# A decoder with routed experts: one fill of unused rows dropped, the buffer moved, full blocks taken first, block loads split over two queues

## The reference, cut to what matters

```python
H, I, E = 256, 256, 8      # width, hidden width, experts
# z: the layer-normed tokens (4 * 512 rows of 256); one expert a token
logits = z @ Wg + bg                        # rows x 8, the largest one is chosen
e = argmax(logits)
out = x + gelu(z @ W1[e] + b1[e]) @ W2[e] + b2[e]
```

## Time and profile before

| | us |
|---|---|
| median of 3 runs | 2154.18 (2151.05 to 2156.48) |
| the profiled execution | 2155.8 |
| its span, first to last instruction | 2154.1 |
| PE busy | 1856.0 (86%) |
| DVE busy | 1631.2 (76%) |
| ACT busy | 1281.1 (59%) |
| POOL busy | 218.6 (10%) |

### The profile page before, as it was taken

One profiled execution on the slowest core, in us unless ns is written; L12 is line 12 of the kernel. 1 busy time (PEld: TensorE's weight loads), 2 busy tenths in 40 slices (PEclk: granted clock), 3 DMA queues, 4 the chain that ended last, 5 costly groups with the idle time before them and its releaser, 6 DMA issues.

```text
span 2154.1 us, 41917 instructions
## 1 busy us (share of the span) xinstructions
PE 1856.0 (86%) x17110; PEld 1031.9 (48%) x17110; DVE 1631.2 (76%) x2621; ACT 1281.1 (59%) x1919; POOL 218.6 (10%) x230
## 2 busy tenths in 40 slices
PE   4999988988999988988899978989899987468947
PEld 2576752324666652423666653323567663023224
DVE  8888878796888878696888768697778878339643
ACT  5666646487566656487566645668566645346912
POOL 1000001300100001300100001020100002003413
PEclk8999999999999999999999999999999999689978
DMA  7477710011477730010367640000277761942034
GB/s 273 74 126 118 133 50 12 9 46 31 82 123 126 125 65 12 9 45 21 79 121 124 115 91 12 9 26 21 62 123 124 124 117 30 127 64 101 2 88 107
DMA packets 454607, 169.51 MB, mean 79 GB/s; under 512 B 428389, under 2 KB 444016, under 8 KB 453904
## 3 DMA queue, kind: packets, MB, share of 16 engines
q1 hardware_dynamic: 449216, 149.29, 34.7%
q0 software_dynamic: 5200, 17.55, 4.9%
HBM read 45.14 MB, written 18.52 MB: 30 GB/s over the span
## 4 chain that ended last, share of the span: by engine, by line
PE 48%; DVE 27%; DMA 12%; ACT 6%; issue 4%; SPq 2%; POOL 1%; POOLq 0%; DVEq 0%; ACTq 0%
DVE nmx L2177 14%; DMA arena<-arena 11%; PE ps L753 8%; PE ps L755 8%; PE ps L754 7%; PE ps L1135 6%; PE ps L1121 3%; PE ps L925 3%; DVE arena L1987 3%; PE ps L919 2%; PE ps L920 2%; PE ps L1085 1%; ACT arena L1497 1%; PE ps L1145 1%; SPq L597 1%
## 5 line engine op out<-in xcount | busy, mean ns | idle before, releaser
L2177 DVE TENSOR_REDUCE nmx<-ps 128x2 f32<-128x1024 f32 x384 | 445.1, 1218 | 51.6 <-PE ps L1085 49.8
L1669 ACT ACTIVATE arena<-ps 128x512 f32<-128x512 f32 x768 | 406.8, 601 | 99.9 <-PE ps L1121 94.9
L1972 DVE TENSOR_SCALAR_CACHE_REDUCE ps<-ps 128x1536 f32<-128x1536 f32 x128 | 225.7, 1763 | 46.4 <-PE ps L755 45.6
L1135 PE MATMUL ps<-arena 128*17 128x256 f32 x3072 | 242.8, 393 | 0.0
L1987 DVE SCALAR_TENSOR_TENSOR arena<-arena,rs 128x1536 f16<-128x1536 f32 x128 | 231.6, 1809 | 4.2 <-ACT arena L1559 4.2
L1559 ACT ACTIVATE arena<-arena,rs 128x1536 f16<-128x1536 f32 x128 | 200.8, 1569 | 42.9 <-DVE rs L1978 42.9
L1121 PE MATMUL ps<-arena 64*128 64x512 f16 x768 | 171.0, 396 | 47.7 <-DMA arena<-arena 45.8
L1550 ACT ACTIVATE arena<-ps,nm 128x1536 f32<-128x1536 f32 x128 | 197.0, 1539 | 15.7 <-DVE ps L1972 15.7
L753 PE MATMUL ps<-arena 128*128 128x512 f16 (+2 forms) x508 | 178.5, 352 | 24.7 <-DMA arena<-zx_d 22.6
L919 PE MATMUL ps<-arena 128*128 128x128 f16 x1536 | 185.3, 219 | 0.8 <-DMA arena<-arena 0.8
L920 PE MATMUL ps<-arena 128*128 128x128 f16 x1536 | 185.3, 219 | 0.0
(11 more groups left out here) (334 smaller groups left out, 3553.7 us busy)
## 6 DMA issues: line engine op xcount, KB each, us to landing
zx_d<-in_eye POOLq DMA_DIRECT2D x7, 1300.0 KB
arena<-in_weights SPq DMA_DIRECT2D x8, 929.0 KB, 18.2
arena<-arena SPq DMA_DIRECT2D x72, 64.0 KB, 2.1
arena<-arena SPq DMA_TRANSPOSE x272, 3.7
arena<-in_ctx SPq DMA_DIRECT2D x4, 1024.0 KB, 5.5
arena<-in_ctx_t SPq DMA_DIRECT2D x4, 1024.0 KB, 4.9
arena<-in_experts SPq DMA_DIRECT2D x1, 3840.0 KB, 11.5
arena<-zx_d SPq DMA_DIRECT2D x23, 132.0 KB, 2.2
```

Source lines behind the costliest of these rows:

```text
L1135: mm(ps[32 * j:32 * j + VW, 7, cols], v17[:, kt, 4 * g_ + j, :], pr_[:, (4 * t + j) % RING, cols], start=(kt + half == 0), stop=(kt == mod ...
L1669: A(pr_[:, n % RING, :], ps[:, 4 + n % 3, :], ACT.Exp).then_inc(b_exp.sem, 1)
L1972: TS_(s_, s_, -XS, None, ALU.mult, ALU.min, accum_out=nm[:, i:i + 1]).then_inc(s_max.sem, 1)
L2177: V.tensor_reduce(nmx[:, g_ % 2, ch, :, pp, i], ps[:, 2 * (z % 2):2 * (z % 2) + 2, :], AX.X, ALU.max, negate=True)\
```

## The change

It has six parts.

- `pad_regions` is gone. In its place SP writes, once and before batch 0's x is loaded, one constant row (all 4096.0, which is no token number) to the first 128 rows of each of the 8 regions, by 8 DMAs. Every expert's rows now start behind these 128 (`held` starts at 128), and `REGION` is 2176 rows and no longer 2432.
- A block that isn't full now ends at the last row of its expert and so reads older rows at its front. `above` gives those rows a number past the end, and the scatter leaves them out.
- `arena` is allocated first and not last. Its first byte in a partition moves from 130528 to 16512. That is 224 above a multiple of 256 before, and 128 above one after; or 32 above a multiple of 64, and on one. `b2` moves into it. The small tables of the experts move into `rope_k`, so that they can be written earlier.
- Five blocks (`OLD`) are surely full with rows of batches 0 to 2: 1536 rows less at most 7 unfinished blocks leave 5. Their table is made by `old_blocks` during batch 3's `cross_attention`, they are loaded as soon as buffers are free, and blocks 0 and 1 are computed ahead of batch 3's routing, blocks 2 to 4 beside or behind it. `new_blocks` makes the table of the other 18.
- Batch 3's z is turned by PE (`transpose_last`, 8 products, ACT copies, DVE subtracts) and not by DMA. Its copy of x (L507 before) is issued behind the first three block transposes.
- SP issues only the block transposes; the plain loads are issued from ACT between the gelus (`load_rows`), three blocks ahead, each behind its wait for the buffer. The row numbers are loaded into registers in two lots (5 and 18) on SP, ACT and PE, and no more one a block.

```diff
-PAD = (NE - 1) * P
-REGION = (B - 1) * S + PAD
+OLD = (B - 1) * S // P - (NE - 1)
+REGION = B * S + P
...
+        arena = sb("arena", [P, ARENA // 4])
         wh, wl = sb("wh", [P, NW], F16), sb("wl", [P, NW], F16)
...
             sp.wait_ge(pad_out.sem, 16)
+            sp.wait_ge(pads_set.sem, 15)
+            for e in range(NE):
+                sp.dma_start(zx_d[REGION * e:REGION * e + P, :], no_row).then_inc(pad_out.sem, 16)
...
-            transpose_rows(B - 1)
-            sp.wait_ge(zx_out.sem, zx_out.at(B, 16 * NE))
-            sp.wait_ge(e_table.sem, e_table.at(0, 1))
-            for j in range(NB):
+            def load_block(j, at):
                 r_ = j % BR
-                at = sp.value_load(where[0:1, 1, j:j + 1], min_val=0, max_val=NE * REGION - P)
                 if j >= BR:
                     sp.wait_ge(e_h.sem, e_h.at(0, 2 * (j - BR)) + 2)
-                    sp.wait_ge(o_out[r_].sem, 16 * (j // BR))
-                rows = zx_d[bass.ds(at, P), :]
-                sp.dma_start_transpose(zb[r_], rows[:, 0:D].bitcast(F16)).then_inc(block_in[r_].sem, 16)
-                sp.dma_start(xb[r_], rows[:, D:ZW]).then_inc(block_in[r_].sem, 16)
+                sp.dma_start_transpose(zb[r_], zx_d[bass.ds(at, P), 0:D].bitcast(F16)).then_inc(block_in[r_].sem, 16)
+            sp.wait_ge(e_table.sem, e_table.at(0, 1))
+            old = rows_at(0, OLD)
+            sp.wait_ge(pv_mm.sem, pv_mm.at(B - 1, 8 * 48))
+            for j in range(OLD - 2):
+                load_block(j, old[j])
+            keep_rows(B - 1)
+            for j in range(OLD - 2, OLD):
+                load_block(j, old[j])
+            sp.wait_ge(e_table.sem, e_table.at(0, 4))
+            new = rows_at(OLD, NB)
+            sp.wait_ge(zx_out.sem, zx_out.at(B, 0))
+            for j in range(OLD, NB):
+                load_block(j, new[j - OLD])
...
-                        if b == B - 1:
-                            pad_regions()
...
             def experts():                                  # PE
+                at = list(weights_at(0, OLD))
+                pe.wait_ge(lx_added.sem, lx_added.at(B - 1, 2 * NT))
+                for j in range(2):
+                    block_hidden(j, at[j])
+                transpose_last()
+                for j in range(2):
+                    block_out(j, at[j])
                 route_logits(B - 1)
+                block_hidden(2, at[2])
                 route_ranks(B - 1)
+                for j in range(3, OLD):
+                    block_hidden(j, at[j])
+                    block_out(j - 1, at[j - 1])
+                pe.wait_ge(e_table.sem, e_table.at(0, 4))
+                at += weights_at(OLD, NB)
...
             def experts():                                  # ACT
                 load_table(3, ACT.Gelu)
+                at = list(rows_at(0, OLD))
+                for j in range(OLD):
+                    load_rows(j, at[j])
+                for j in range(2):
+                    gelus(j)
+                for c in range(DC):
+                    act.wait_ge(n_t.sem, n_t.at(B, c + 1))
+                    A(yT[0][:, c, :], ps[:, LAST_BANK[c], :], ACT.Copy).then_inc(n_hi.sem, 1)
                 rows_hi(B - 1)
+                for j in range(2, OLD):
+                    gelus(j)
+                act.wait_ge(e_table.sem, e_table.at(0, 6))
+                at += rows_at(OLD, NB)
+                act.wait_ge(zx_out.sem, zx_out.at(B, 0))
+                for j in range(OLD, OLD + 3):
+                    load_rows(j, at[j])
+                for j in range(OLD, NB):
+                    gelus(j)
+                    if j + 3 < NB:
+                        load_rows(j + 3, at[j + 3])
...
             def experts():                                  # DVE
                 normalise(B - 1, 4, x, zf)
+                for j in range(2):
+                    split_block(j)
+                for c in range(DC):
+                    dve.wait_ge(n_hi.sem, n_hi.at(B, c + 1))
+                    TT(yT[1][:, c, :], ps[:, LAST_BANK[c], :], yT[0][:, c, :], ALU.subtract).then_inc(n_lo.sem, 1)
+                for j in range(2):
+                    finish_block(j)
+                route_choice(B - 1)
                 rows_lo(B - 1)
-                route_choice(B - 1)
                 route_slots(B - 1)
-                block_tables()
-                for j in range(NB + 1):
+                new_blocks()
+                for j in range(2, NB + 1):
```

More of the change, by code:

```diff
@@ L216, in decoder @@
         caff_first = Layout(81920).take([4, S])
+        no_row = Layout(92160).take([ZW])
+        b2 = Layout(95232).take([D])[0:NE]
         xn = Layout().take([NT, D])
-        zTt = [Layout(32768 if b == B - 1 else 4096).take([4 * NT, P], F16) for b in range(B)]
+        zTt = Layout(4096).take([4 * NT, P], F16)
         zf = Layout(77824).take([NT, D])
@@ L1757, in next_window, with gelus, rows_at @@
                 context_hi(t)
+            def gelus(j):
+                if j >= 2:
+                    act.wait_ge(e_split.sem, e_split.at(0, j - 1))
+                for m in range(DC):
+                    act.wait_ge(e_h.sem, e_h.at(0, 2 * j + m + 1))
+                    A(hg[:, j % 2, m, :], ps[:, HID_BANK[j % 2][m], 0:P], ACT.Gelu, bias=bias1[:, j, m:m + 1]).then_inc(e_gelu.sem, 1)
+            def rows_at(j0, j1):
+                return nc.values_load_multi_w_load_instructions(where[0:1, 1, j0:j1], engines=(mybir.EngineType.Activation,),
+                                                                min_val=0, max_val=NE * REGION - P)[1]
@@ L2359, in across, with count_rows @@
                 return v_.unsqueeze(1).to_broadcast([P, n, v_.shape[-1]])
-            def along(v_):
-                return v_.unsqueeze(2).to_broadcast([P, NB, NE])
-            def block_tables():
-                many, blocks, ends = cnt[:, 0], cnt[:, 1], cnt[:, 2]
+            blocks, ends, skip, many = (cnt[:, k] for k in range(4))
+            def count_rows():
                 own.link(STT(many, count_up[:, 0:NE], -1.0 * REGION, held[:], ALU.mult, ALU.add))
+                own.link(TS_(many, many, -1.0 * P, None, ALU.add))
@@ L2374, in block_tables @@
-                own.link(V.tensor_reduce(ends, upto, AX.X, ALU.add))
-                past, owner, first, count, room, home, at = (bs[:, k] for k in range(7))
-                own.link(TT(bt[:, 0], along(count_up[:]), across(ends, NB), ALU.is_ge))
-                own.mark(V.tensor_reduce(owner, bt[:, 0], AX.X, ALU.add))
-                own.link(TT(bt[:, 1], bt[:, 0], across(blocks, NB), ALU.mult))
-                own.mark(V.tensor_reduce(first, bt[:, 1], AX.X, ALU.add))
-                own.link(TS_(home, owner, NE - 1.0, 1.0 * REGION, ALU.min, ALU.mult))
@@ L2394, in block_tables @@
-                own.link(STT(room, past, -1.0 * P, count, ALU.mult, ALU.add))
-                own.link(TS_(bs[:, 7], room, token[:, 0:1], 2.0 * B * S, ALU.is_le, ALU.mult))
+                own.link(STT(blocks, blocks, ROUND, skip, ALU.subtract, ALU.subtract))
+                running(ends, blocks)
+                table(OLD, NB, blocks, False)
             def split_block(j):
```

240 lines of the change are left out of this document (146 added, 94 removed).

## The result

| | before | after |
|---|---|---|
| median of the runs, us | 2152.61 (4 runs, 2149.02 to 2156.48) | 2082.70 (4 runs, 2078.69 to 2087.81) |
| ratio, 95% interval | | 0.9676 [0.9648, 0.9704] |
| span of the profiled execution, us | 2154.1 | 2076.8 |
| mean granted clock | 0.961 | 0.982 |

The change saves 70 us by the medians and 77.3 us between the two profiled executions. The 77.3 us are taken apart here by milestones that both traces have. A number with "FR" counts from the last layer norm of the last sequence: POOL's rstd at 2054.26 before and at 1998.76 after.

What follows compares the result with a forecast made beforehand. The prediction saw batch 3's shifts queued behind the fill, the serial piece before the first block, and the 23 blocks as bounds. 49.4 - 1.0 + 17.0 = 65.4 us saved gave 2088.8 us, range 2073 to 2101.

Steps and rivals of the forecast that it cites:

- (1): Batch 3's `self_attention`: without the fill, rstd pair 79 us apart as in batch 2, no DMA wait over 3 us; 49.4 us saved.
- (2): Start of batch 0: the eight filling DMAs delay x, which lands at about 55; 1.0 us lost.
- (3): Batch 3's routing: choice near 2062 less 49, slots 2 to 4 us earlier than before on the same count.
- (4): Loop head: block 5's first product about 3 us (3.4) later than block 0's was, ACT reading row numbers just ahead.
- 0.30 us and 18 times 0.16 us, 3.2 us: Ahead of block 5's plain load: ACT's price for reading its 18 row numbers.
- (5): Block loop: 2.2 us steps at full clock, PE never waiting for a transpose of `zx_d`; 17 steps in 41.1 us.
- 2.43 less some 0.2: Block loop: PE loses its own value load, so a block takes 2.2 us at full clock.
- in-order wait of ACT for scatters: Block loop: three steps take 6.2 us at the median landing, 2.1 each, so PE still bounds; 2.7 at worst landings.
- rival B: Block loop: blocks get no faster, through longer scatter landings or half clock; only 7 us saved there, 2099 us; chance 0.20.
- (6): Transposes of `latent` still land in 3.7 us; the buffer's place brings 0, bounds 2 us lost and 16 gained.
- such a fifth: SBUF-to-SBUF transfers in all batches: a fifth off 85 us of moving data gains 17 us, giving 2072; rival's chance 0.13.
- Rival D: Block loop: ACT's loads serialise it, steps of 10 to 12 us; slower than before, 2218 at 10 us; chance 0.01.

Runs made afterwards that it cites:

- e1: The changed kernel with the fill put back as eight transfers (11.2 MB) into a scratch tensor nobody reads: 2138.43 us.
- e5: The changed kernel without the bounds checks behind its register reads, the reads of 18 values kept: 2082.17 us.
- e4: The changed kernel with row numbers and weight offsets of blocks 5 to 22 read singly before use on SP, ACT and PE: 2082.60 us.
- e8: The changed kernel with single reads on SP and ACT, and PE reading four values ahead of block 5, then two ahead of each block: 2082.54 us.
- e3: The changed kernel with the plain loads issued by SP again and no row numbers read on ACT: 2083.49 us.
- e6: The changed kernel with three early blocks in place of five, 20 in place of 18 after the choice: 2097.20 us.
- e2: The changed kernel with `arena` allocated last again, its base back at 32 past a multiple of 64: 2082.19 us.
- e10: The changed kernel with spread reads and seven block buffers in place of six, bounds checks kept: 2083.93 us.
- e9: The changed kernel with spread reads and no bounds checks, six block buffers: 2076.53 us.
- e11: The changed kernel with spread reads, no bounds checks and seven block buffers in place of six: 2076.46 us.
- e7: The changed kernel with the fill put back at half its rows (5.6 MB) into the scratch tensor: 2108.30 us.

## Why the prediction was right, point by point

**(1) The fill: right.** 50.3 us for 49.4, no DMA wait of PE left between the pair, and e1 brings it back with its four waits. That batch 2 served as the measure for batch 3 was the safest step of the whole: the two agree to 0.01 us after. That "PE, DVE and ACT all stood still" was too strong, since PE was busy 7.37 of 20 us and DVE 7.78; the price didn't rest on it.

**(2) The start: right.** 1.1 us for 1.0; x landed, and was used at once, at 56.16, where I had said about 55.

**(3) The choice: right in direction, too small.** "Slots 2 to 4 us earlier on the same count" came out at 5.4. I had reckoned with TensorE at half clock for much of this; the row of 2003.8 to 2008.8 us (from ahead of the choice to the slots; columns as in the earlier trace rows, the clock is 1.00) says otherwise:

```profile
2003.80:2008.80 5.00, 3.46 (x62) 2.88 (x60) 4.53 (x19) 1.91 (x5) 2.06 (x2) 1.00 0.16 56
```

**(4) Block 5: right in direction, by two errors that offset each other.** The forecast was 3.4 us later than block 0 had been, and it is 5.0. The term "0.30 us and 18 times 0.16 us, 3.2 us" was mis-sized: it is 3.7 uncovered and 18 times 0.225 and more, 8.1 us. I had taken the load's price from a read of one value for a read of 18, and the register operation without what follows it. Against that, the gelu of block 4 ended at FR + 21.6 and not at 25.0. e5 confirms both halves of the term; e4 and e8 show that the reads' price, once moved, is paid by PE in the loop.

**(5) The loop: mechanism right, size off.** 2.15 us a step for 2.42. PE is the bound in most of it, at 1.8 to 1.9 us and not 2.2 at full clock, and only the stretch at its beginning is at half clock. The term at fault is "2.43 less some 0.2" for PE's own value load: e4, which puts that read back, has 2.45 us a block, so the read is worth 0.6 us and not 0.2. The in-order wait of ACT for scatters, which I had priced at the median landing as just not binding, does bind three times (3.0 to 4.1 us, landings up to 3.9). So part of rival B is real and the other part (the clock) isn't; on the whole steps got faster, and B is out. Which part of the change made them faster is only in part shown: e4 shows it for PE's read, e3 doesn't show it for the plain loads, and no run puts the turn of z on PE back or prices the early blocks cleanly (e6). "PE never waiting for transposes" holds: of its two waits for `zx_d` in the last 60 us, 9.8 us in all, 9.5 are for block 5's plain load behind ACT's reads, as the chain has it.

**(6) The buffer's place: right.** Transposes at 3.7 us, e2 at the same time. The Trainium skill (DMA: Bandwidth & Descriptors, section "How a descriptor splits into AXI transactions") lets a read begin at the 256-byte boundary below its start, by which the change spares a fifth of the beats (an estimate from that rule). With the prediction's price for such a fifth e2 would stand some 17 us higher, and it stands 0.5 us lower, so the runs don't bear it out that these transfers are bound by their beats. What sets the 3.7 us is open.

**What is left.** 6.2 us were saved ahead of the fill that I hadn't forecast. FR's spread of 8 us between executions of nearly the same code is as large, so I claim no cause. The profiled executions differ by 77.3 us and the medians by 70, because the one before lay 3.2 us above its median and the one after 4.0 below. Between the traces the forecast of 65.4 us is 11.9 short: 6.2 ahead of the fill, 0.9 at the start, the fill and up to FR, and 4.8 behind FR (-1.6 for the late block 5, 4.6 for the loop, 1.8 for the end). By the medians it is 4.5 short. That these small errors and the spread of the executions leave so little is in part luck; what the forecast had right is the fill, 49.4 of its 65.4 us. Rival D is out: the loop didn't serialise.

## What to carry to other kernels

A transfer in the background is not free where small ones on the path queue behind it: look for the same stretch in a repetition without it, and the difference is its price, here 50 us for 11.2 MB. A value that steers addresses costs the engine that reads it, per value and per check, and where that engine bounds the loop moving the read didn't hide it (e4, e8); here only taking the checks off and spreading the reads together brought 6 us, and either alone, or one engine fewer that reads (e3), brought nothing that the runs can tell. Before pricing a saving at a loop's head, see which engine bounds the loop: five variants (e3, e4, e5, e8, e10) brought its start forward by 2.4 to 6.9 us, and none of them ended sooner by more than the runs can tell; only e9 and e11 (8.6 and 7.8 us), with spread reads and no checks, did.

## What the runs showed of the hardware that I had not expected

- A read of values into registers grows with their number: 0.28 to 0.30 us for one value and 4.05 to 4.53 us for 18 in one instruction, on ACT, SP and PE (the change, e4 and e5), and on PE 0.53 for two and 1.01 for four (e8, e9), plus 0.225 us a value for the check. Per value a long read (0.23 us) costs as much as the check.
- The granted clock is 1.00 in the 5 us of small products around the choice (PE busy 3.46 of 5.00), and 0.67 in the six behind them (2008.8 to 2014.8 us), where PE is idle.
- The stall from the fill is nearly in proportion to its size: 23.6 us for 5.6 MB, 54.3 for 11.2 MB (e7 and e1), with the DMA engines busy to a share of 0.96 in a stretch of 20 us.
